# A decoder layer with mixture of experts: the last batch worked tile by tile, twelve more expert weight pairs loaded early, and unused products in PE's waits

## What is computed

```python
x = layernorm(x + attn(x))          # 16 heads of 16, rotary; softmax attention and a
                                    # linear-memory read, mixed by a gate for each head
x = layernorm(x + xattn(x, ctx))    # queries from rmsnorm(x), 64 context tokens, masked softmax,
                                    # output times sigmoid(x @ wg.T)
x = layernorm(x + moe(x))

def moe(x):                         # 1024 tokens, E = 64 experts, K = 8, INNER = 96, CAP = 64
    probs = softmax(x @ gate_w.T)
    w, sel = top_k(probs, K);  w = w / sum(w)
    # the first CAP tokens of an expert, in order of token, get a slot; later ones are dropped
    xin[expert, slot] = x[token]
    out = (silu(xin @ wg) * (xin @ wu)) @ wd
    y[token] += out[expert, slot] * w
```

## Time and profile before

| | |
|---|---|
| median of 3 runs | 418.92 us (418.79 to 421.54) |
| the profiled execution | 416.79 us, its span 415.0 us |
| mean granted TensorE clock | 0.829 of full speed |
| busy, share of the span | PE 64%, DVE 56%, POOL 39%, ACT 31% |
| moved by DMA | 66.61 MB, mean 161 GB/s |

### The profile page before, as it was taken

The page is one execution under the profiler, slowest core; times in us unless marked ns, Lnnn a source line. Parts: engine busy times, 40 slices in busy tenths (PEclk is TensorE's granted clock), DMA queues, the critical chain, the costliest instruction groups (busy, mean ns, idle before and its releaser), DMA issues.

```text
span 415.0 us, 5198 instructions
## 1 busy us (share of the span) xinstructions
PE 265.8 (64%) x1680; PEld 166.5 (40%) x1680; DVE 230.4 (56%) x519; ACT 130.3 (31%) x230; POOL 163.7 (39%) x165
## 2 busy tenths in 40 slices
PE   4748766599896958877659693620089999960000
PEld 4635535366574626664345432310045555420000
DVE  0747553568777649668462845150057777540393
ACT  5300382007930039511096204010024444230022
POOL 2220022300227742247700287127606478477073
PEclk9897899679997799988969969565579999995555
DMA  7699999970192320962200299200069998966791
GB/s 260 168 133 345 358 386 195 260 206 2 38 134 92 133 86 2 118 111 105 73 2 0 76 343 318 70 25 9 1 194 300 318 192 175 309 99 69 265 383 66
DMA packets 47261, 66.61 MB, mean 161 GB/s; under 512 B 5979, under 2 KB 33241, under 8 KB 47234
## 3 DMA queue, kind: packets, MB, share of 16 engines
q1 hardware_dynamic: 39120, 56.52, 49.3%
q0 software_dynamic: 7680, 9.47, 11.5%
q10 hardware_dynamic: 434, 0.27, 0.2%
HBM read 36.45 MB, written 28.75 MB: 157 GB/s over the span
## 4 chain that ended last, share of the span: by engine, by line
PE 28%; issue 19%; DVE 15%; DMA 12%; ACT 10%; another core or an unknown queue 6%; POOL 5%; SPq 3%; POOLq 0%; DVEq 0%; ACTq 0%
PE M L1052 11%; PE O L1052 6%; DMA acc_d<-xp_t,idx_out 5%; PE SA L1052 3%; DMA early<-early 3%; ACT probs L530 3%; SPq L343 3%; POOL xin_d L451 3%; DVE nmax L763 2%; PE SB L1052 2%; PE O L1398 2%; DVE early L1012 1%; DMA early<-acc_d 1%; ACT xp L553 1%
## 5 line engine op out<-in xcount | busy, mean ns | idle before, releaser
L451 POOL DMA_INDIRECT xin_d<-row,idx_slot x64 | 63.2, 988 | 24.7 <-issue 18.8
L489 POOL DMA_INDIRECT acc_d<-xp_t,idx_out x32 | 49.4, 1544 | 34.5 <-DVE idx_out L988 15.1
L471 POOL TENSOR_TENSOR early<-early 128x1024 f32<-128x1024 f32 x4 | 8.5, 2133 | 86.3 <-ACT early L540 86.3
L1052 PE MATMUL SA<-early 96*128 96x256 bf16 (+1 forms) x128 | 24.4, 325 | 20.1 <-ACT early L594 9.5
L1052 PE MATMUL SB<-early 96*128 96x256 bf16 (+1 forms) x128 | 23.9, 319 | 6.4 <-DVE nmax L763 5.0
L763 DVE TENSOR_REDUCE nmax<-SA 128x4 f32<-128x1024 f32 x16 | 19.5, 1218 | 13.2 <-PE SA L1052 13.2
L1398 PE MATMUL O<-con,probs 128*128 128x128 f32 x40 | 9.2, 319 | 26.2 <-DMA probs<-xin_d 26.2
L1052 PEld LDWEIGHTS SA<-early 96*128 96x128 bf16 (+1 forms) x128 | 12.3, 110 | 31.5 <-issue 12.4
L763 DVE TENSOR_REDUCE nmax<-SB 128x4 f32<-128x1024 f32 x16 | 19.5, 1220 | 9.6 <-PE SB L1052 5.3
L659 ACT ACTIVATE xp<-M 128x96 f32<-128x96 f32 x32 | 8.0, 251 | 51.8 <-PE M L1052 47.8
L1052 PE MATMUL O<-xf,early 128*128 128x256 f32 x64 | 18.6, 445 | 6.4 <-DMA early<-weights 5.2
(11 more groups left out here) (201 smaller groups left out, 644.3 us busy)
## 6 DMA issues: line engine op xcount, KB each, us to landing
gu_sb<-wgu SPq DMA_DIRECT2D x20, 384.0 KB
acc_d<-zeros SPq DMA_DIRECT2D x3, 2176.0 KB, 19.0
early<-early SPq DMA_DIRECT2D x48, 128.0 KB, 5.4
early<-acc_d SPq DMA_DIRECT2D x24, 256.0 KB, 7.5
xin_d<-zeros SPq DMA_DIRECT2D x1, 5136.0 KB, 23.2
early<-wgu SPq DMA_DIRECT2D x12, 384.0 KB
wd_sb<-wd SPq DMA_DIRECT2D x20, 192.0 KB
probs<-xin_d SPq DMA_DIRECT2D x20, 160.5 KB
```

Source lines behind the costliest of these rows:

```text
L451: nc.gpsimd.indirect_dma_start(xin_d, bass.IndirectOffsetOnAxis(ap=idx_slot[:, t, k:k + 1], axis=0), row[:, t, :], None, bounds_check=SLOT ...
L471: nc.gpsimd.tensor_tensor(rest[:], qk[:], parts[:, :, 0], ALU.subtract).then_inc(S["rest_r"], 1)
L489: nc.gpsimd.indirect_dma_start(acc_d[p % CHAINS], bass.IndirectOffsetOnAxis(ap=idx_out[:, p:p + 1], axis=0), yw[:, p % YRING, :], None, bo ...
L1052: return nc.tensor.matmul(o, l, r, start=start, stop=stop)
```

## The change

- **Memory.** The cross-attention's weights and buffers, which had places of their own, are carved from a second block `middle`. It later takes twelve more weight pairs (19 to 30, `MID`). SP issues them after the last slot numbers and ahead of the first gathers. Only pair 31 is left to follow into the ring.
- **Last batch.** `last_batch` replaces `iteration(None, B - 1, None)` on each engine. Each step handles one tile, with PSUM banks of its own, and tile 1's steps lie between those of tile 0. POOL fits the norm's scales between the indirect DMAs of batch 2, and writes tile 0's rows of batch 3 when its indices are there. The rows and indices of batch 3 have buffers of their own (`row_last` in `att_f`, `idx_last`).
- **POOL.** `xk_blk` for the next batch is built at the end of a round, ahead of the second norm's scale, no longer ahead of `into_slots`.
- **PE.** `spare_products` multiplies ones into a bank whose values are not used: 3 products of 512 columns before `first(2)`, 7 before `first(3)` in each of the three full rounds, and 9 between `memory_products` and `memory_read` in (1,0,2) and (2,1,3). The first ones wait for `eprob` and `pval` of the batch before, which free that bank.

```diff
 GU_W, WD_W = 2 * 2 * NC * INNER, 2 * D
...
         early = sb("early", [P, LATE * (GU_W + WD_W)])
...
         def place(p):
 
             if RING <= p < RING + LATE:
                 return late_gu[:, p - RING], late_wd[:, p - RING]
-            r = p if p < RING else (p - LATE) % RING
+            if MID_FROM <= p < MID_TO:
+                return mid_gu[:, p - MID_FROM], mid_wd[:, p - MID_FROM]
+            r = p if p < RING else (p - LATE - MID) % RING
             return gu_sb[:, r], wd_sb[:, r]
...
-            iteration(None, B - 1, None)
+            last_batch(B - 1)
...
-                if b is not None and a is None:
-                    need(sp, "o_mm", b)
-                    for p in range(RING, RING + LATE):
-                        load_pair(sp, p)
...
+            def last_batch(b):
+                need(sp, "res1", b)
+                sp.dma_start(xt[:], x_tok[b + 1]).then_inc(S["xt_in"], 16)
+                need(sp, "o_mm", b)
+                for p in range(RING, RING + LATE):
+                    load_pair(sp, p)
+                rows_out(b, row_last)
...
+            need(sp, "idx_slot", B - 1, NT)
+            for p in range(MID_FROM, MID_TO):
+                if (p - MID_FROM) % LATE_GRP == 0:
+                    g = (p - MID_FROM) // LATE_GRP
+                    sp.wait_ge(S["late"][g], late_count(g))
+                load_pair(sp, p)
...
+            def context_keys(b):
+
+                prev(pool, "x_mm", b)
+                for n in range(NC):
+                    nc.gpsimd.tensor_tensor(
+                        xk_blk[:, n], xk_f[:, n, bass.ds(b, 1), :].broadcast_to([P, HC, MEM]),
+                        con[:, CONST["xhead_of_row"]].unsqueeze(2).broadcast_to([P, HC, MEM]), ALU.mult
+                    ).then_inc(S["kblk"], 1)
...
                     norm_scale(b, 1)
-
-                    pool.wait_ge(S["xk_ev"], 1)
-                    pool.wait_ge(S["consts"], 16)
-                    prev(pool, "x_mm", b)
-                    for n in range(NC):
...
+                    if b == 0:
+                        pool.wait_ge(S["xk_ev"], 1)
+                        pool.wait_ge(S["consts"], 16)
+                        context_keys(b)
                     if b >= 1:
-                        into_slots(b - 1)
+                        rows_ready(b - 1)
+                        into_slots(b - 1, idx_slot, row, range(NT))
...
                 if b is not None:
+                    context_keys(b + 1)
                     norm_scale(b, 2)
...
+            def last_batch(b):
+                norm_scale(b, 1)
+                rows_ready(b - 1)
+                into_slots(b - 1, idx_slot, row, (0,))
+                into_slots(b - 1, idx_slot, row, (1,), range(0, 3))
+                norm_scale_of(b, 0)
+                into_slots(b - 1, idx_slot, row, (1,), range(3, 5))
+                norm_scale_of(b, 1)
+                into_slots(b - 1, idx_slot, row, (1,), range(5, TOPK))
+                for t in range(NT):
+                    need(pool, "idx_slot", b, t + 1)
+                    need(pool, "wrow", b, t + 1)
+                    need(pool, "x2", b, t + 1)
+                    need(pool, "keycol", b, 1)
+                    into_slots(b, idx_last, row_last, (t,))
+
...
+                    moved("x1_mm", x1_f, work_of(t)[:, 0, 0:D], "x1_ev", t)
+                for t in range(NT):
+                    moved("xq_mm", xq_f, work_of(t)[:, 1, 0:D], "xq_ev", t)
+                prev(act, "ygate", b)
+                need(act, "rstd", b, 1)
+                weights_exp(0)
+                gate_tanh(0)
+                weights_moved(0)
+                weights_exp(1)
+                gate_tanh(1)
+                moved("rsum_mm", rsum_f, work_of(0)[:, 1, D:2 * D], "rsum_ev", 0)
+                weights_moved(1)
+                moved("rsum_mm", rsum_f, work_of(1)[:, 1, D:2 * D], "rsum_ev", 1)
+                for t in range(NT):
+                    moved("x2_mm", x2_f, scores_of(t)[:, 0, 0:D], "x2_ev", t)
+                for t in range(NT):
...
+                normalized(b, 1, x1, "x1")
+                dve.wait_ge(S["first_key"], 1)
+                need(dve, "keycol", b - 1)
+                nc.vector.tensor_copy(row_last[:, :, D + E], keycol[:]).then_inc(S["keycol"], 1)
+                less_max(0)
+                less_max(1)
+                weight_sum(0)
+                weight_scale(0)
+                weight_sum(1)
+                context_out(0)
+                weight_scale(1)
+                residual(0)
+                context_out(1)
+                moments(0)
+                residual(1)
+                moments(1)
+                router_max(0)
+                chosen(0)
+                router_max(1)
+                slots(0)
+                chosen(1)
+                slots(1)
...
+            def spare_products(n, bank):
+
+                for _ in range(n):
+                    mm(M[:, bank, :], ones_sq[:], ones_sq[:].unsqueeze(1).broadcast_to([P, 4, P]))
+
...
                 if a is not None:
                     first(0)
                     first(1)
+                    if b is not None:
+                        prev(pe, "eprob", b)
+                        prev(pe, "pval", b)
+                        spare_products(3, 1)
                     first(2)
...
                 if a is not None:
+                    if b is not None:
+                        spare_products(7, 1)
                     first(3)
                     first(4)
                 if b is not None:
...
                 if c is not None:
                     memory_products()
-                if c is not None:
+                    if b is not None:
+                        spare_products(9, 0)
                     memory_read()
...
+                prev(pe, "eprob", b)
+                prev(pe, "pval", b)
+                queries(0)
+                queries(1)
+                scores(0)
+                scores(1)
+                tokens_projected("xg", x1_f, "gate_mm", 0)
+                weights_turned(0)
+                tokens_projected("xg", x1_f, "gate_mm", 1)
+                weighted(0)
+                weight_sums_turned(0)
+                weights_turned(1)
+                context_out(0)
+                weighted(1)
+                weight_sums_turned(1)
+                turned("res2", scores_of(0)[:, 0], res, "x2_mm", 0)
+                context_out(1)
+                router_scores(0)
+                turned("res2", scores_of(1)[:, 0], res, "x2_mm", 1)
+                router_scores(1)
+                prev(pe, "sel_sum", b)
+                slot_counts(0)
+                slot_counts(1)
```

More of the change, by code:

```diff
@@ L112, in build @@
         kfeat_tok = carve([NT, D])
-        memory = sb("memory", [P, NC, HC * HV])
+        memory = carve([NC, HC * HV], of="middle")
         q_op = carve([NH, T], BF16)
@@ L378, in _ @@
                 load_rows(p)
-            follows = {(p - LATE - RING if p - LATE - RING < RING else p - RING): p for p in range(RING + LATE, PAIRS)}
+            follows = {p - MID_TO: p for p in range(MID_TO, PAIRS)}
             for p in range(PAIRS):
```

316 lines of the change are left out of this document (244 added, 72 removed).

## The result

The changed kernel takes 405.57 us (median of 4 runs, 404.55 to 407.82) against 420.23 (4 runs, 418.79 to 423.12) for the kernel before in the same set: a ratio of 0.9695, 95% interval 0.9649 to 0.9741. It is faster, by 14.7 us; I had forecast 398 with a range that ends at 405. Its profiled execution took 406.08 us with a span of 404.2, so 10.8 us of span went, where my sum had 20.5.

The account below looks back on a forecast made before the run. PE and DVE bound the rounds, single engines in turn the last batch, then POOL, PE and scatter landings. Gains of 4.2 + 7.1 + 9.2 = 20.5 us gave 398 us from a 418.92 median, range 391 to 405.

Parts of the forecast that it names:

- Spare products and `xk_blk`: Full rounds: spare products hold PE's clock and the moved build starts POOL's streams 2.1 us earlier; 4.2 us saved.
- Last batch by tiles: Last batch: overlapping two tiles puts tile 1's indices at 269, 8.7 us earlier, with 2 us left for late posts.
- Rival 1: Last batch: late posts at every hand-over of the tiled chain, 446 us at 3.57 us each; chance 0.04.
- First gather: Before the expert rounds: queued behind the weight loads, it lands at about 295.2 instead of 302.3, 7.1 us earlier.
- Expert rounds: Expert rounds: scatters meet gathers alone, PE's pace of 2.0 us a pair counts; 66.2 us instead of 75.4, 9.2 saved.
- Rival 3: Expert rounds: gathers, not weights, slow the scatters, so only 2 us are gained; 405 to 406 us, chance 0.10.
- rival 4: Last batch doesn't get shorter: POOL's order and late posts eat the overlap, 0 to 2 us gained; 404, chance 0.10.
- rival 5: All stretches work better: no late posts, faster weight loads, quicker last three pairs; 391 us, chance 0.14.
- rival 2: Full rounds: the clock is not held, rounds gain nothing and (1,0,2) loses 2.6 us; 405 us, chance 0.12.

Follow-up runs that it names:

- a3: Changed kernel with the indirect DMAs of batches 0 and 1, and the waits for them, left out; 391.69 us, ratio 0.9325.
- d1: The changed kernel itself run again, on a chip where the kernel before takes 400.42 us; 384.53 us, ratio 0.9617.
- a4: Changed kernel with each 16-DMA stream in the rounds cut into two eights, the second behind PE's turned maxima; 399.33 us, ratio 0.9493.
- b1: a4 without the spare products; 404.59 us, ratio 0.9631.
- d2: The kernel of a4 run again, on the chip of d1; 383.5 us, ratio 0.9587.
- b2: a4 with no middle weight pair ahead of the gathers, one behind the gather of each expert round 0 to 11; 400.7 us, ratio 0.9499.
- b3: a4 with four middle pairs ahead of the gathers and eight paced by expert rounds 0 to 7; 398.73 us, ratio 0.9456.
- d3: The kernel of c2 run again, on the chip of d1; 379.62 us, ratio 0.9496.
- b4: a4 with the 24 loads of the middle pairs issued by ACT instead of SP; 398.07 us, ratio 0.9421.
- a2: Changed kernel with the twelve middle pairs issued behind the first ten gathers instead of ahead of them; 426.76 us, ratio 1.0147.
- c2: a4 with eight middle pairs ahead of the gathers and four in expert rounds 1, 4, 7 and 10; 380.05 us, ratio 0.9439.
- e2: d3 without the spare products, where the kernel before takes 421.25 us; 398.12 us, ratio 0.9459.

## Why the forecast was 7 us too low

Point by point, by the prediction's own steps.

*Spare products and `xk_blk`, 4.2 us: failed, 2.0 came.* The mechanism of the clock was right: the windows at 129 to 140 are at 1.00 and `xq` took 1.9 us. (In before the fall that I put at 129.7 is at 129.4 in finer windows, which changes nothing.) (1,0,2) behaved as taken, at full level from 82; of the 1.3 us up to its `memory_read` 1.0 was forecast. The two rounds behind it gave 0.3 and 0.5 us instead of 2.0 and 2.1. What failed is the sentence that the move of `xk_blk` "is what lets the round keep PE's gain". The stream did start 2.0 us earlier after `memory_read`, and DVE's copy of the turned maxima came 1.9 and 1.8 us earlier after it. The tanh came 0.9 us later in (2,1,3) and 0.5 earlier in (3,2,-), and PE's second scores 0.9 and 0.5 us earlier. So on this kind of chip the held posts, not PE, set when ACT and DVE go on, and PE's gain became a wait (posts 6.7 and 8.2 us late at the tanh, against 3.7 and 6.3 before). In (2,1,3) the clock fell behind it, where before stood at the full level from 140 to 180, and PE's first eight second scores at half speed took back 0.4 us of that. How exactly a post is tied to the stream isn't known: in the trace of before the tanh of batch 1 began 2.0 us ahead of the stream's end at 151.01, in the changed kernel it began 0.9 us behind it. a3 and d1 show the cause: without the stream, or with it on a chip that holds no posts, the same two rounds take 49.8 and 44.4 us instead of 55.5 and 51.0. I had the rows in hand: the tanh of batch 2 in the earlier trace rows, 6.3 us behind PE's product, which I booked as a fact of the last third of the stream and not as the bound of the round.

*Last batch by tiles, 8.7 us: 6.9 came.* The term was mis-sized by the late posts, which I put at 2 us. d1, where none is late, needs 27.94 us for the stretch, the changed kernel 35.71 in its profile, so on this kind of chip the tiled chain lost up to 7.8 us. ACT lost 1.48 and 1.80 us at two of its waits; most of the rest goes with the clock, at the half level behind them and at the full one in d1:

```profile
254.00:268.00 14.00, 9.41 (x45) 6.40 (x45) 8.49 (x41) 2.38 (x6) 6.86 (x9) 0.50 0.48 136
...
235.00:244.00 9.00, 5.39 (x42) 3.62 (x41) 6.34 (x28) 2.95 (x6) 6.13 (x9) 1.00 1.04 307
```

Without late posts I had forecast 31.9 from the residual to the indices; the tiled chain itself is 4 us better than my count. Rival 1, a late post at every hand-over, didn't come: two were late.

*First gather, 26.2 us after the indices: 30.8 came, and this is the largest miss.* I let the weights bound it, with the 25.7 us of the earlier 24 loads, and let the gather land 0.5 us behind the last of them. The loads' own time was right in the traces where their end can be read (a4, b1, d1, d2: about 26 us behind the indices). But the gather is only issued when the last indirect DMA has landed, and that took 7.48 us beside the full engines instead of 2.1 (I had it landed at about 291, it was 294.87); then the gather took 4.62 instead of 2.28. What I missed is the chain of two landings: the first comes at about the end of the loads, and the gather, which I let ride along for 0.5 us, follows it with 2.2 to 4.6. b2, b3 and d3 show it: with no load in flight the two take 4.2 to 4.4 us together. In the profile of the changed kernel the loads were slower as well:

```profile
293.00:299.00 6.00, 0.00 (x0) 0.00 (x0) 0.00 (x0) 0.00 (x0) 0.00 (x0) 0.50 1.05 266
```

There the rate doesn't fall before 299, and from 271 to 291 it was 263 GB/s, against 287 in the same 20 us behind the indices in d1. Why, no run shows. b4 shows that the order in SP's queue, on which I had argued, is not the cause here, though a2 shows that the order costs dearly where it is wrong.

*Expert rounds, 9.2 us: 8.3 came.* Pace 2.0, hardly a wait for a scatter, last landing in 3.77: the mechanism was right, the size 0.9 us off.

*Rivals 3 to 5.* Rival 3 (gathers alone slow the scatters) didn't come: 62.1 us from the first to the last scatter. Nor did rival 4, as the last batch did get shorter, or rival 5. My rival 2 ("The clock is not held") named the right sum, 405, for the wrong reason.

So of the 9.7 us that are missing from the sum, 2.2 lie in the rounds, 1.8 in the last batch, 4.6 ahead of the first gather, 0.9 in the expert rounds and 0.2 in the end. The first two come from held posts and the clock behind them. That share goes with the chip: d1, the same kernel, is 20 us faster in the three stretches where POOL streams. But before is as much faster on those chips (400 to 402 us against 420), so the change is worth 15 to 16 us on either kind.

Open is what on a chip holds PE's posts behind a stream of POOL, and why three of the five chips do it and two don't. No trace names the releaser, or tells whether PE posts late or the others see it late. Also untried is d3_split_eight on a chip of the first kind. It is the fastest kernel of both sets in which it ran (0.9496 and, as c2, 0.9439, against 0.9617 for the changed kernel), and its two parts, a4's cut and pairs ahead that are through in time, each helped on the first kind (a4, and e2 against b1). What the spare products are worth on the second kind was not tried either.

## What to carry to other kernels

Before crediting a gain to an engine, look at what releases the next one: where a wait has no named releaser and ends with another engine's stream, shorten or cut that stream first; only then does a held clock pay (nothing measurable uncut, between 2 and 10 us cut). Transfers put ahead "for free" in idle DMA time must be through before the small transfer on the critical path is issued: twelve pairs made the first gather 5 to 7 us later, eight cost nothing there. And run the kernel before on every chip on which you run anything, since it took 400 us on one and 421 on another.

## What the hardware showed that I had not expected

- PE's posts to ACT and DVE came up to 6.7 and 8.2 us late during an unbroken stream of 16 indirect DMAs on POOL (1.28 us apart), 2.4 and 3.9 us with 8 in a row (a4, b4), on the three chips where before took 420 us; never on the two where it took 400 to 402.
- An indirect DMA of small rows landed in 2.1 us with the DMA engines free and in 6.6 to 7.5 us with weight loads in flight, whether SP or ACT had issued them.
- Weight loads beside POOL's stream moved at 263 GB/s over 20 us of the changed kernel's profile, with the engines full, and at 283 to 290 in a4, b1, d1 and d2.
- A pair of expert weights loaded in each expert round cost 0.7 us a pair (b2, where a scatter landed in 8.45 us, and b3); one in every third round 0.1 to 0.3 in d3 and 0.6 to 0.7 in c2.
